# A one-layer decoder block on one core: the output projection as three float32r products, with its transposed input split by ScalarE and VectorE

## The reference, cut to what matters

```python
def attn(x, Wq, Wk, Wv, Wg, Wo):          # 8 heads of 128, on layernorm(x)
    q = l2norm((x @ Wq).reshape(B, T, H, DK)); k = l2norm((x @ Wk).reshape(B, T, H, DK))
    v = (x @ Wv).reshape(B, T, H, DV);         alpha = sigmoid(x @ Wg).reshape(B, T, H, DK)
    # scan over time: S = alpha_t * S + k_t v_t^T ;  o_t = q_t S
    return o.reshape(B, T, H * DV) @ Wo                       # Wo is 1024 x 256
x = x + attn(layernorm(x), Wq, Wk, Wv, Wg, Wo)
x = x + cross_attention(layernorm(x), ctx, W)     # softmax((x) (ctx W^T)^T) ctx, 16 x 128 x 256
x = x + moe_ffn(layernorm(x), ...)                # top 2 of 8 experts per sequence, gelu
```

## Time and profile before

| | value |
|---|---|
| runs | 562.89, 564.17, 567.42 us |
| the profiled execution | 563.17 us, span 561.4 us |
| TensorE matmuls | 488.9 us busy (87%) |
| TensorE weight loads | 407.4 us busy (73%) |
| VectorE | 383.1 us busy (68%) |
| ScalarE | 356.9 us busy (64%) |
| POOL | 85.1 us busy (15%) |
| mean granted TensorE clock | 0.951 |
| DMA | 20.35 MB, mean 36 GB/s |

### The profile page before, as it was taken

One profiled execution on the slowest core, in us unless ns is written; L12 is line 12 of the kernel. 1 busy time (PEld: TensorE's weight loads), 2 busy tenths in 40 slices (PEclk: granted clock), 3 DMA queues, 4 the chain that ended last, 5 costly groups with the idle time before them and its releaser, 6 DMA issues. The chain is left out here.

```text
span 561.4 us, 25935 instructions
## 1 busy us (share of the span) xinstructions
PE 488.9 (87%) x11232; PEld 407.4 (73%) x11232; DVE 383.1 (68%) x1069; ACT 356.9 (64%) x825; POOL 85.1 (15%) x71
## 2 busy tenths in 40 slices
PE   1798999999988999899988999899988999775616
PEld 1587888888877888787867888688867887664415
DVE  4588887766786888765686887765775888614541
ACT  4667787766758677567758677577748676442202
POOL 1012111111111111410111111410111111300020
PEclk9999999999999999899999999899989999997557
DMA  8800000001010100210010100210000100201021
GB/s 334 252 3 5 4 4 4 4 4 40 4 41 2 41 4 4 77 41 22 23 40 5 40 4 4 78 40 22 23 2 4 40 5 4 78 0 39 0 75 37
DMA packets 15264, 20.35 MB, mean 36 GB/s; under 512 B 1200, under 2 KB 12976, under 8 KB 15152
## 3 DMA queue, kind: packets, MB, share of 16 engines
q1 hardware_dynamic: 13872, 14.49, 7.6%
q0 software_dynamic: 1280, 4.20, 2.6%
HBM read 16.60 MB, written 2.10 MB: 33 GB/s over the span
## 5 line engine op out<-in xcount | busy, mean ns | idle before, releaser
L438 ACT COPY states<-states 128x512 f32<-128x512 f32 (+1 forms) x160 | 94.6, 592 | 95.3 <-DVE states L646 88.6
L363 POOL TENSOR_TENSOR rnorm<-norm_sq,neg_half 128x8 f32<-128x8 f32 (+1 forms) x33 | 53.8, 1631 | 291.0 <-DVE norm_sq L686 291.0
L646 DVE TENSOR_TENSOR states<-states,spans 128x512 f32<-128x512 f32 x128 | 88.5, 691 | 12.2 <-DVE states L646 4.6
L1128 PE MATMUL acc<-wo_sb,oT_sb 128*128 128x256 f32 x256 | 63.8, 392 | 8.2 <-ACT oT_sb L465 8.2
L1030 PE MATMUL ring<-xnT,wk_sb 128*128 128x512 f32 x192 | 55.7, 429 | 8.9 <-DVE v_sb L695 6.0
L1043 PE MATMUL ring<-wv_sb,xnT 128*128 128x256 f32 x384 | 57.5, 302 | 0.6 <-DVE wv_sb L877 0.6
L1128 PEld LDWEIGHTS acc<-wo_sb,oT_sb 128*128 128x128 f32 x256 | 46.0, 189 | 15.3 <-ACT oT_sb L465 9.3
L1030 PE MATMUL ring<-xnT,wq_sb 128*128 128x512 f32 x192 | 53.1, 412 | 1.7 <-ACT rowsT L469 1.0
L677 DVE COPY_PREDICATED blocks<-owned,lo_bank 128x128 f32<-128x128 uint32 x128 | 38.5, 301 | 20.2 <-PE lo_bank L1053 14.8
L1043 PEld LDWEIGHTS ring<-wv_sb,xnT 128*128 128x128 f32 x384 | 50.9, 200 | 1.1 <-DVE wv_sb L877 0.7
L1030 PE MATMUL ring<-xnT,wg_sb 128*128 128x512 f32 x192 | 51.0, 402 | 0.0
(11 more groups left out here) (145 smaller groups left out, 852.4 us busy)
## 6 DMA issues: line engine op xcount, KB each, us to landing
x_buf<-x_dram SPq DMA_DIRECT2D x4, 512.0 KB, 4.2
ctxT_sb<-ctxT_dram SPq DMA_DIRECT2D x8, 256.0 KB, 3.4
ctx_sb<-ctx_dram SPq DMA_DIRECT2D x4, 512.0 KB, 4.8
out_dram<-x_mid SPq DMA_DIRECT2D x8, 256.0 KB, 2.1
states<-wk_dram SPq DMA_DIRECT2D x1, 1024.0 KB, 6.1
states<-wg_dram SPq DMA_DIRECT2D x1, 1024.0 KB, 8.1
states<-wq_dram SPq DMA_DIRECT2D x1, 1024.0 KB, 10.1
v_sb<-wv_dram SPq DMA_DIRECT2D x1, 1024.0 KB, 11.7
```

The costliest lines, as they stand in the source:

```text
L363: nc.gpsimd.tensor_tensor(rnorm[:, m % 4, first:last], norm_sq[:, first:last], neg_half[:, first:last], ALU.pow).then_inc(rnorm_set, 1)
L438: nc.scalar.copy(dst, src).then_inc(carry_set, 1)
L646: nc.vector.tensor_tensor(dst, src, by, ALU.mult).then_inc(decayed, 1)
L1128: last = mm(accs[z][:, D * m:D * m + D], oT_sb[:, n % 2, T * b:T * b + T], wo_sb[:, h], start=(h == 0 and m == 0), stop=(h == H - 1 and m ...
```

## The change

`wo_sb` holds an upper and a lower float32r part. Wo is loaded into `sel` (not used until the first gather of expert rows), and POOL makes both parts from it, a copy and a subtraction of 128x2048, after its first three power operations. ScalarE's copy of the transposed head output writes the upper half of `oT_sb` in float32r, for every head; a new VectorE step, `oT_lower`, subtracts it from the bank and writes the lower half. The output projection waits for this step (`oT_lo_set`) in place of ScalarE's copy and has three matmuls for each sequence in place of one. `ctxT_sb` becomes a view of `ctx_sb`, so that both are loaded by turns, and `downT` a view of `xn`.

```diff
-        wo_sb = sb("wo_sb", [P, H, D])
+        wo_sb = sb("wo_sb", [P, 2, H, D], F32R)
-        ctxT_sb = sb("ctxT_sb", [P, KC, GB, T])
+        ctxT_sb = ctx_sb[:].rearrange("p (c b) (h t) -> p c (b h) t", c=KC, t=T)
-        oT_sb = sb("oT_sb", [P, 2, N])
+        oT_sb = sb("oT_sb", [P, 2, N], F32R)
-        downT = sb("downT", [P, GB, KC, P])
+        downT = xn[:].rearrange("p b (c n) -> p b c n", c=KC)
+        stage_o = view(sel, 0, [[1, H * D]])
...
-                        "o": (o_set, n + 1), "oT": (oT_set, n + 1)}[kind]
+                        "o": (o_set, n + 1), "oT": (oT_lo_set, n + 1)}[kind]
...
-            sp.dma_start(wo_sb[:], wo.rearrange("(h p) n -> p h n", p=P)).then_inc(w_in, 16)
+            sp.dma_start(stage_o.rearrange("p (h n) -> p h n", h=H), wo.rearrange("(h p) n -> p h n", p=P)).then_inc(wo_in, 16)
             load_ctxT(0)
-            load_ctx(0)
 
             for i in range(1, NG):
                 sp.wait_ge(tail_mm, TAIL["keys", i - 1, 1])
-                load_ctxT(i)
+                load_ctx(i - 1)
...
                 sp.wait_ge(tail_mm, TAIL["cross", i - 1, 1])
-                load_ctx(i)
+                load_ctxT(i)
+            sp.wait_ge(tail_mm, TAIL["keys", NG - 1, 1])
+            load_ctx(NG - 1)
...
             reciprocal_norms(-1)
+            pool.wait_ge(wo_in, 16)
+            upper, lower = (wo_sb[:, part].rearrange("p h n -> p (h n)") for part in (HI, LO))
+            nc.gpsimd.tensor_copy(upper, stage_o).then_inc(wo_hi, 1)
+            pool.wait_ge(wo_hi, 1)
+            nc.gpsimd.tensor_tensor(lower, stage_o, upper.bitcast(F32), ALU.subtract).then_inc(wo_split, 1)
...
-                nc.scalar.copy(oT_sb[:, n % 2], ring_of(("oT", n))[:]).then_inc(oT_set, 1)
+                nc.scalar.copy(oT_sb[:, HI], ring_of(("oT", n))[:]).then_inc(oT_set, 1)
...
+            def oT_lower(n):
+                dve.wait_ge(oT_set, n + 1)
+                nc.vector.tensor_tensor(oT_sb[:, LO], ring_of(("oT", n))[:], oT_sb[:, HI].bitcast(F32),
+                                        ALU.subtract).then_inc(oT_lo_set, 1)
...
-                        ln_normalize(("mid", t), x_mid, ("x3T", t - 1, 1) if t > 0 else ("xT", 1, 1))
+                        ln_normalize(("mid", t), x_mid, ("hid", t - 1, 0) if t > 0 else ("xT", 1, 1))
...
                     q_decayed(n + 1)
+                if n >= 2:
+                    oT_lower(n - 2)
                 tail_part(n, "late")
...
+            oT_lower(U - 2)
             o_scaled(U - 1)
             tail_part(U, "end")
+            oT_lower(U - 1)
...
-                pe.wait_ge(oT_set, n + 1)
+                pe.wait_ge(oT_lo_set, n + 1)
...
-                    last = mm(accs[z][:, D * m:D * m + D], oT_sb[:, n % 2, T * b:T * b + T], wo_sb[:, h],
-                              start=(h == 0 and m == 0), stop=(h == H - 1 and m == 1))
+                    for part, (a, w) in enumerate(PARTS):
+                        last = mm(accs[z][:, D * m:D * m + D], oT_sb[:, a, T * b:T * b + T], wo_sb[:, w, h],
+                                  start=(h == 0 and m == 0 and part == 0), stop=(h == H - 1 and m == 1 and part == 2))
```

17 lines of the change are left out of this document (9 added, 8 removed).

## The result

The changed kernel takes 590.28 us (median of 4 runs, 588.29 to 592.46), the kernel before took 563.53 us beside it (561.87 to 567.42): ratio 1.0465, 95% interval 1.0396 to 1.0534. On another chip it was 584.12 against 557.64, ratio 1.0479 (1.0410 to 1.0548). The forecast had the direction (slower) and not the size: +26.7 us where it said +10.9, and outside its range of 562 to 583.

A forecast was written before the change was run, and what follows sets the result against it. Matmuls set the pace in passes 4 to 8, a VectorE and ScalarE chain leads passes h = 2 to 6. Sum -0.5 + 3.6 + 3.6 + 3.2 + 1.0 = +10.9 us: 575.0 us, range 562 to 583.

The forecast's parts named there:

- POOL, said +1.0: Start of the kernel: POOL's Wo split takes at least 4.2 us; between 0 and 1.6 reaches TensorE, taken as 1.0.
- The cover of 2.6 us: First passes: slack from VectorE's decay 2 to its reader plus 0.77 us of VectorE idle, hiding part of POOL's split.
- The projection's gain, said -10.6: Output projection: holds TensorE 1.50 us in place of 1.83, so 32 heads gain 10.6 us.
- less 0.33: Each head's projection: 0.33 us shorter, subtracted from the delay at projections in the pass-by-pass sum.
- the walk: Pass-by-pass delays along TensorE's list and the VectorE and ScalarE chain: -0.5 us first group, +3.6 second and third, +3.2 last.
- direct waits: Projections wait for VectorE's new subtraction where their lead over ScalarE's copy is under 0.79 us: 10.2 us in all.
- the pushing: Passes h = 2 to 7: the step delays VectorE's following line, masked copies and decays by 0.61 to 1.0 us.
- The last group, said +3.2: Pass 26 to the loop's end: starts with no delay, no next x to normalize; costs 3.2 us.
- three signs of being wrong: Pass 10 to 18 stretch not longer; subtraction clearly off 0.69 us; or passes 4 to 8 not shorter.
- Rival 3: POOL holds VectorE 3 us more and TensorE's clock falls in three more places: 583.4 us; chance 0.15 with the fourth.
- Rival 4: Projection: weight loads set its length, so it isn't shortened and 10.6 us are missing: 585 us; 0.15 with the third.
- Rivals 1 and 2: First: delays don't carry over, 564.8 us, chance 0.20. Second: gain kept, most waits vanish, 553.6 to 557, chance 0.10.

The follow-up runs named there:

- pool_split: Kernel before with the shared space, plus POOL's copy and subtraction of 128x2048 into a tile nobody reads; projection in float32: 571.49 us, ratio 1.0102.
- no_lower: Changed kernel without VectorE's subtraction; the third product repeats the upper half of the output, so twelve matmuls a head stay: 573.0 us, ratio 1.0129.
- no_lower_no_pool: Changed kernel with Wo split by ScalarE and VectorE, without VectorE's subtraction of the output; twelve matmuls a head stay: 566.35 us, ratio 1.0010.
- split_act_dve: Changed kernel with Wo's split off POOL: ScalarE copies the upper part, VectorE subtracts in four pieces: 582.55 us, ratio 1.0290; again 582.41, 1.0290.
- shared_space: Kernel before with only the shared space (ctxT and downT as views, loads in changed order); float32 projection, no step, no split: 565.88 us, ratio 0.9997.
- dve_step: Kernel before with the shared space, plus VectorE's subtraction for every head and the float32 projection's wait for it; no POOL work: 581.46 us, ratio 1.0288.
- warm: Kernel with twelve matmuls, no subtraction and no POOL split, plus 8 filler matmuls in passes 10, 18 and 26: 559.11 us, ratio 1.0028 to before.
- step_late: Changed kernel with Wo split by ScalarE and VectorE, subtraction behind the next head's decays, projection behind the attention product: 717.45 us, ratio 1.2906 to before.

## Why the prediction was wrong in size

1. **POOL, said +1.0, measured +6 to +7.** This is the largest single miss of a cost. Passes 0 and 1 are 6.6 us longer, the kernels with and without POOL's steps differ by 5.9 us (`pool_split`) and 6.7 us (`no_lower` against `no_lower_no_pool`); the changed kernel and `split_act_dve` differ by some 10 us with an interval of 4 each way. The failed step is "If VectorE stood still for all 4.2 us, 1.6 would reach TensorE; if it doesn't, 0. I take 1.0". The length was too short (1.89 + 4.89 = 6.78 us; the memset of the earlier trace rows was no measure for a subtraction with two inputs), and VectorE stood still for 5.9 us of it. The cover of 2.6 us was there and more: TensorE's wait for the held decays is only 2.3 us (2.08 and 0.20). What the term left out is the rest: TensorE's clock fell (0.82 against 0.93) and made its work in these passes 2.9 us longer (23.73 against 20.83), and it stalled for 1.97 us in front of the squared norms of pass 0. That stall is in all four profiles with POOL's two long instructions and in none without; its cause stays open. The page "SBUF — State Buffer", "SBUF: two separate sides", of the Trainium skill was right that such instructions exclude each other whole: the decays ended with POOL's instructions, and with pieces they took turns. The subtraction took 4.89 us where the page "GPSIMD Engine Reference" has 4.5, and the prediction's estimate of 6.6 us for both steps (with 2.1 from the memset) came close to 6.78. The forecast had both rules in a sentence beside the sum and set a row of another kind of operation above them.

2. **The projection's gain, said -10.6, measured about 0.** Its length was right (1.53 for 1.50); the step "32 of them by 10.6 us" failed as a gain of the kernel, and with it "less 0.33" in the walk. With the step it is 1.0290 against 1.0288, without it 1.0010 against 0.9997. The passes show where it goes. I compare the means of the three profiles with the long projection and no step (`before`, `shared_space`, `pool_split`) and of the two with the short one (`no_lower`, `no_lower_no_pool`). Passes 5 to 9, 12, 16, 17, 20, 24, 25 and 28 get shorter by 0.2 to 0.4 us each, 3.8 us in all. Passes 10 and 18 get longer by 0.8 each, and 14, 22, 29, 30 and the last stretch (from v of head 31 to the last projection) by 0.3 or 0.4; with so few profiles a single pass can be chance. So the gain does arrive in many passes and is lost again in others. Passes 10 and 18 are those in which TensorE waits for v_scaled, and pass 10 above shows how an earlier arrival becomes a longer wait. The clock takes at most some 3 us; what takes the rest, pass by pass, stays open. The prediction had said itself that the chain leads the passes h = 2 to 6, and still counted gains in them. The 19 us of the earlier trace rows in which TensorE is busy for 18.49 are mainly pass 12 and part of pass 13; the one got shorter by 0.3, the other by less than 0.1, so the busy share doesn't tell which passes hand a gain on.

3. **The step, in the forecast 10.2 us of direct waits and then the pushing, measured 16.4 in all.** The forecast never priced it apart from the gain. Its sum with all of the gain put back is 10.9 - 1.0 + 10.6 = 20.5 us, and less by the gains that the walk didn't count, so it was too much by up to 4, and the errors partly cancel; that is luck. The cause named was half right: the waits come (21.4 us in 16, forecast over 10 in some 15), but they are at most a small part of the price, since without any such wait the time is the same within its interval. The price is VectorE's queue, as the walk had it. The walk itself was good for a group: from the wait for v_scaled in pass 10 to that in pass 18 it is 130.19 us (168.56 to 298.75) for 125.59 before (160.89 to 286.48), +4.6 for a forecast +3.6.

4. **The last group, said +3.2, measured +8.7.** Pass 26 grows by 1.5, 27 by 0.9, 29 by 0.7, 30 by 2.2 us, and the stretch from v of head 31 to the last projection by 3.6. The term mis-sized is "the same walk gives 3.2, with the end of the loop in it": pass 30 and the last stretch alone make 5.8, where the walk had 0.74 less 0.33 for head 30. The step alone shows most of it (`dve_step` 110.1 us against `shared_space` 103.3). Of the last stretch 1 to 2 us may belong to the one execution of before: it took 25.0 us there, wholly at the upper clock, and 26.1 and 27.1 in the other two with the long projection and no step, at 0.93 and 0.87; it is 0.88 in the changed kernel.

5. **The first weights came 2.1 us later**, which no term foresaw. The first weight copy stood at 11.4 and 11.2 us in two profiles of the changed kernel and at 9.2 before. In the seven profiles in which Wo goes to its own tile it stands at 8.8 to 9.2; in the twelve in which Wo is loaded into the memory of `sel` it stands four times at 8.8 to 9.6 and eight times at 10.3 to 11.4, and in one kernel once at 11.0 and once at 8.8. So loading Wo into `sel` goes with it but doesn't always bring it; by what way stays open.

Of the three signs of being wrong that the prediction named none came in full, and the range was missed all the same. 1.50 us for the projection held, passes 5 to 8 are shorter by 0.29 to 0.44 us as said (pass 4 isn't, 12.98 for 12.58), VectorE's busy time grew by 26.6, where 22 was said, and the 4.6 over it are mostly the time for which POOL held it. One reading of the prediction is loose: passes 4 to 8 take 12.4 to 14.0 us before, not about 12.4 each; nothing rests on it. Rival 3 named both mechanisms that were missing, POOL's hold and the clock, and at 583 was the nearest in kind; it still counted the projection's gain. Rival 4 came near in its number (585) for a wrong reason: the projection did get shorter. Rivals 1 and 2, in which TensorE's gain survives, fell.

The parts add up: 16.4 for the step, 6 to 7 for POOL, 0 to 1 for projection and shared space make 22 to 25 us; measured were 26.7, with an interval of some 4 each way. The pair of kernels that gives 10 for POOL can't be added here, as it is the changed kernel itself less the others.

## What to carry to other kernels

A shorter matmul is worth what is left of it at the next wait for another engine, and a stage in which the matmul engine looks 97% busy doesn't tell that: take work off the matmul engine in an experiment and see how much of it comes through (here 3 of 16 us) before a shorter matmul is paid for with a step on VectorE. The price of an instruction is its place: 0.69 us of VectorE cost 0.5 us each on average in front of the masked copies, nothing there in the passes in which VectorE would have idled, and 0.04, give or take 0.1, in a gap one step earlier. Moving a copy back behind the one that others wait for won 4 us with no work saved. A long POOL instruction that reads tiles is to be priced as if VectorE, where it reads two tiles of SBUF, stood still for its whole length, with TensorE's clock on top, unless nothing waits for VectorE then.

## What was not expected of the hardware

TensorE's 64 squared-norm matmuls stall at issue while POOL issues the gathers of expert rows, on some chips only. It is the second line of the waits above: of its 14 times twelve, 5.3 us in sum and 0.5 us each for the most part, stand beside the gathers in passes 14, 22 and 30. In the kernel before it looks like this, with a gather of POOL from 228.79 to 230.16 and the next from 230.47:

```profile
230.23 0.32 PE L1100 MATMUL hi_bank<-ones,squares 128*32 128x1 f32 x10 [0.49 <-issue]
231.00 0.26 PE L1100 MATMUL hi_bank<-ones,squares 128*32 128x1 f32 x4 [0.45 <-issue]
```

All 16 profiles of the other groups have six to sixteen such stalls. The three of the chip of the third group (`warm`, `step_late` and the changed kernel again) have none, though in two of them the gathers run beside the same matmuls. In `warm` the line of the waits, which is a stall of pass 1, is this:

```profile
PE hi_bank L1122 <- issue: 0.5, 1, 0.5
```

Pass 14 took 13.87 us there, 16.44 before on the first chip; for the changed kernel it was 15.61 and 18.63. Passes 14, 22 and 30 together take 41.2 us in `warm` and 50.0 in `no_lower_no_pool`, which has the same work in them. The kernel before took 557.64 us on that chip and 563.5 to 567 on the others, so these three passes can make up the difference. Ratios were hardly touched by it (1.0479 and 1.0465). What in the chip makes the difference wasn't tried.

Taking turns costs as well: POOL's work takes 6.78 us in two instructions that keep VectorE out, and 12.1 us in sixteen that don't, while VectorE's four decays are still 0.25 us longer (3.15 for 2.90) and its four span products 1.2 us (2.17 for 0.99). Over all, the pieces won back 5.6 us, give or take 4, of the 10 that the ratios give POOL.
